# Two chained cross-head projections: TensorE as four 64x64 arrays, data laid out by halves, column matrices kept in SBUF, the result added in place

## What is computed

```
ret  = einsum('BGMTS,GMN->BGNTS', x, w + eye)
hq   = einsum('BGMTS,BTGIM->BGITS', x, qw1);  ret += einsum('BGITS,BTGIM->BGMTS', hq, qw2)
hk   = einsum('BGMTS,BSGIM->BGITS', x, kw1);  ret += einsum('BGITS,BSGIM->BGMTS', hk, kw2)
ret += x * qdd[t] + x * kdd[s]
```

## Time and profile before

| | |
|---|---|
| median of three runs | 987.55 us |
| profiled execution | 987.69 us, of which the span of the instructions is 985.8 us |
| TensorE (matmul) | 946.6 us busy, 96% of the span |
| VectorE / GpSimd / ScalarE | 748.4 / 715.7 / 319.2 us busy |
| DMA | 159.74 MB, 16 engines busy 50.5% of the span by queue q1 |

### The profile page before, as it was taken

The page is one execution under the profiler, slowest core; times in us unless marked ns, Lnnn a source line. Parts: engine busy times, 40 slices in busy tenths (PEclk is TensorE's granted clock), DMA queues, the critical chain, the costliest instruction groups (busy, mean ns, idle before and its releaser), DMA issues.

```text
span 985.8 us, 24446 instructions
## 1 busy us (share of the span) xinstructions
PE 946.6 (96%) x8378; PEld 939.4 (95%) x8378; DVE 748.4 (76%) x1036; ACT 319.2 (32%) x514; POOL 715.7 (73%) x603
## 2 busy tenths in 40 slices
PE   3679999999999999999999999999999999999998
PEld 3669999999999999999999999999999999999998
DVE  3996767787777876788677886779767786778997
ACT  0234333323333333333333233333333333333320
POOL 2998876678766976669866787668876697665666
PEclk8789999999999999999999999999999999999999
DMA  8952118770386506872088702866048730784017
GB/s 214 328 142 61 16 47 296 258 185 1 129 292 240 125 1 210 287 245 43 1 288 288 202 6 86 282 253 164 1 167 286 255 73 1 243 293 128 1 44 299
DMA packets 76493, 159.74 MB, mean 162 GB/s; under 512 B 39936, under 2 KB 40960, under 8 KB 73856
## 3 DMA queue, kind: packets, MB, share of 16 engines
q1 hardware_dynamic: 76416, 158.54, 50.5%
HBM read 89.19 MB, written 69.34 MB: 161 GB/s over the span
## 4 chain that ended last, share of the span: by engine, by line
PE 88%; POOL 7%; DMA 2%; issue 2%; POOLq 1%; DVE 0%
PE PB L482 24%; PE PA L482 23%; PE PA L488 21%; PE PB L488 20%; POOL WA L160 3%; POOL PROD L265 2%; DMA RT<-products 2%; POOL PROD L269 1%; DMA products<-RT 1%; POOL PROD L272 0%; DVE WA L448 0%; POOLq L288 0%; POOLq L160 0%; DVE RT L375 0%; POOLq L283 0%
## 5 line engine op out<-in xcount | busy, mean ns | idle before, releaser
L160 POOL TENSOR_TENSOR WA<-RT,mask 128x512 f32<-128x512 f32 x277 | 341.9, 1242 | 151.1 <-PE PA L482 121.2
L160 POOL TENSOR_TENSOR WA<-RS,mask 128x512 f32<-128x512 f32 x256 | 328.2, 1292 | 104.8 <-PE PA L488 87.3
L482 PE MATMUL PA<-X,WA 128*128 128x128 f32 x2048 | 281.9, 280 | 26.4 <-POOL WA L160 19.5
L482 PEld LDWEIGHTS PA<-X,WA 128*128 128x128 f32 x2048 | 257.2, 192 | 31.5 <-issue 23.9
L405 DVE TENSOR_TENSOR OUT<-PB,X 128x512 f32<-128x512 f32 x256 | 176.0, 691 | 131.2 <-PE PB L482 130.0
L488 PE MATMUL PA<-Y,WA 128*128 128x128 f32 x2048 | 267.9, 272 | 5.9 <-POOL WA L160 5.9
L488 PE MATMUL PB<-X,WB 128*128 128x128 f32 x2048 | 267.5, 272 | 0.0
L338 ACT ACTIVATE Y<-PA 128x512 f32<-128x512 f32 (+1 forms) x256 | 162.1, 633 | 321.6 <-PE PA L482 321.6
L344 ACT ACTIVATE X<-PA 128x512 f32 x256 | 155.6, 608 | 311.1 <-PE PA L488 311.1
L488 PEld LDWEIGHTS PA<-Y,WA 128*128 128x128 f32 x2048 | 247.2, 188 | 7.3 <-POOL WA L160 7.2
L482 PE MATMUL PB<-Y,WB 128*128 128x128 f32 x1880 | 250.3, 274 | 0.0
(11 more groups left out here) (32 smaller groups left out, 62.9 us busy)
## 6 DMA issues: line engine op xcount, KB each, us to landing
X<-in_x_dram SPq DMA_DIRECT2D x128, 512.0 KB, 4.9
out_dram<-OUT SPq DMA_DIRECT2D x128, 512.0 KB, 3.1
RT<-products SPq DMA_DIRECT2D x16, 1024.0 KB, 11.8
OUT<-in_right_dram SPq DMA_DIRECT2D x2, 1024.0 KB, 11.0
products<-PROD SPq DMA_DIRECT2D x16, 128.0 KB, 4.1
Y<-in_right_dram SPq DMA_DIRECT2D x1, 1024.0 KB, 22.9
X<-in_right_dram SPq DMA_DIRECT2D x1, 1024.0 KB, 26.8
QP<-in_rows_dram SPq DMA_DIRECT2D x8, 80.0 KB, 3.4
```

Of the source, the lines that this page charges most:

```text
L160: engine.tensor_tensor(dst, r, m, ALU.mult).then_inc(ready, 1)
L482: last = nc.tensor.matmul(bank[:, r, :], weights[:, r].rearrange("q n p -> q (n p)"), row(buf, pair, r), start=True, stop=True)
```

## The change

TensorE is addressed as four 64x64 arrays: input half h (partitions 0 to 63 or 64 to 127) and output half o. The partitions now hold 2 halves x 4 parts x 16 channels. The row tile of 64 partitions is multiplied by a 64x64 matrix with 4 repeats. Each former matmul of 128 moving columns becomes four of 64 (one per array), which together cover the same row. The results of the two input halves go to two PSUM banks, those of the output halves to the two halves of the partitions.

```
+            def four(banks, at, weights, moving, full=None):
+                for h in range(HALVES):
+                    inside = slice(HALF * h, HALF * (h + 1))
+                    for o in range(HALVES):
+                        rhs = moving(inside, o)
+                        dst = banks[h][HALF * o:HALF * (o + 1), ROWS * at:ROWS * (at + 1)]
...
+                        last = nc.tensor.matmul(dst, weights(inside, o), rhs, start=True, stop=True)
+                if full is not None:
+                    last.then_inc(full, 1)
+            def multiply_rows(banks, weights, rows, full):
+                for r in range(CHUNK):
+                    four(banks, r,
+                         lambda inside, o: weights[inside, r].rearrange("q a n -> q (a n)"),
+                         lambda inside, o: rows[inside, r // PAIR, WIDE * o:WIDE * (o + 1), r % PAIR],
+                         full if r == CHUNK - 1 else None)
```

```
+            def t1_copies(k, e, j):
+                act.wait_ge(a_full, before_t1(k) + j + 1)
+                for h in range(HALVES):
+                    nc.scalar.activation(half_rows(y_rows(e, j), h), by_rows(PA[j % RING][h]), ACT.Copy
+                                         ).then_inc(a_done, 1)
+            def add_rows(k, e, o):
+                dve.wait_ge(b_full, before_t2(k) + o + 1)
+                dve.wait_ge(a_done, copied(before_t1(k + 1)))
+                for h in range(HALVES):
+                    at = half_rows(x_rows(e, t2_chunk(o)), h)
+                    nc.vector.tensor_tensor(at, by_rows(PB[o % RING][h]), at, ALU.add).then_inc(b_done, 1)
```

VectorE only adds from now on. The expanded column matrices RSX are made once and stay in SBUF: layer 1 by ScalarE (16 copies scaled by the mask), layer 2 by GpSimd (4 spreads of 128x2048). GpSimd makes all row matrices, t1's into WA and t2's into WB, in turn, and forms the products once per two blocks, in the middle of the first of the two t phases:

```
+            def turn(m, first, more):
+                k = 2 * m
+                for j in range(CHUNKS):
+                    t1_weights(k + 1, j, False)
+                    t2_weights(k, j, first)
+                    if j == SLOTS - 1 and more:
+                        products_of(m + 1, False)
```

The compact column matrices are formed in 16 units: TensorE broadcasts the k2 values into PSUM by a matmul with a selection matrix (`fill`), VectorE multiplies and adds (`column_unit`), onto a base that GpSimd (layer 1) and ScalarE (layer 2) make. X is double (X[0], X[1]); t2 is added in place into X, stored from there, and the chunk of the block after next is loaded into the same place once the store has landed:

```
+                def reload(o):
+                    j = t2_chunk(o)
+                    sp.wait_ge(stored[j], DMA * (k + 1))
+                    load_x(k + 2, e, j)
+                for o in range(CHUNKS):
+                    sp.wait_ge(b_done, copied(before_t2(k) + o + 1))
+                    store(k, e, t2_chunk(o))
+                    if more and o >= BEHIND:
+                        reload(o - BEHIND)
```

More of the change, by code:

```diff
@@ L21 @@
 CHUNK2 = CHUNK // PAIR
-PER_CHUNK = CHUNK // GRP
-SLACK = 3
+PAIRS = ROWS // PAIR
+SLACK = 1
+RING = 2
 SLOTS = 4
+LAG = 2
+BEHIND = 3
+QUARTERS = 4
+QUARTER = COLS // QUARTERS
+NARROW = QUARTER // HALVES
+UNITS = LAYERS * QUARTERS * RANK
+FILLS = 4
 PARAMS = 2 * RANK * CH + CH
@@ L27 @@
 FLAT = CHUNK * COLS
[L28 to L32, removed]
+BANK = 512
 def cross_conv_kernel(nc, x, first_rows, row_params, col_left, col_right, w, products, out):
@@ L153, in by_columns, with column_index @@
         def by_columns(bank):
[L154 to L159, removed]
+            return bank[:, :].rearrange("q (s a c) -> q s a c", s=CHUNK, c=PAIR)
+        def column_index(o, v):
+            return QUARTER * (v // NARROW) + NARROW * o + v % NARROW
@@ L226, in _ @@
[L226 to L232, removed]
-            sp.wait_ge(first_stored, DMA)
-            load_rt(BLOCKS, 0)
-            load_x(0, 2)
-            load_x(0, 3)
@@ L257, in _ @@
+            load_rt(1, 0, 1)
+            with sp.Fori(0, TURNS - 2) as m:
+                turn(m, True)
+                load_q(m + 2)
+            turn(TURNS - 2, True)
+            turn(TURNS - 1, False)
+            for j in range(CHUNKS):
+                sp.wait_ge(stored[j], DMA * BLOCKS)
         @block.gpsimd
@@ L280, in products_of @@
                     row_matrices(l, (RANK + 1) * (LAYERS * step + l))
-            def phase(compact, before, start, end, there, count):
-                with pool.Fori(start, end) as it:
-                    pool.wait_ge(there, count)
-                    for i in range(RING):
-                        pool.wait_ge(a_full, before + RING * it + i - RING + 1)
-                        spread(nc.gpsimd, WA[:, i], compact, GRP * (RING * it + i), wa_ready)
-            def s2_weights(k, more):
-                if more:
-                    phase(RS[:, 1], before_s2(k), 0, PROD_TURN, rs_ready, LAYERS)
-                    products_of(k + 1)
-                    phase(RS[:, 1], before_s2(k), PROD_TURN, GROUPS // RING, rs_ready, LAYERS)
-                else:
-                    phase(RS[:, 1], before_s2(k), 0, GROUPS // RING, rs_ready, LAYERS)
@@ new lines, in s2_copies @@
+            def s2_copies(k, e, g):
+                act.wait_ge(a_full, before_s2(k) + g + 1)
+                for h in range(HALVES):
+                    nc.scalar.activation(half_columns(X[e], h, g), by_columns(PA[g % RING][h]), ACT.Copy
+                                         ).then_inc(a_done, 1)
+            act.wait_ge(wi_ready, LAYERS)
+            base(1)
+            for j in range(CHUNKS):
+                t1_copies(0, 0, j)
+                if j % 2:
+                    column_spread(j // 2)
@@ new lines, in turn @@
+            def turn(m, more):
+                k = 2 * m
+                for g in range(CHUNKS):
+                    s2_copies(k, 0, g)
+                for j in range(CHUNKS):
+                    t1_copies(k + 1, 1, j)
+                for g in range(CHUNKS):
+                    s2_copies(k + 1, 1, g)
+                if more:
+                    for j in range(CHUNKS):
+                        t1_copies(k + 2, 0, j)
+            with act.Fori(0, TURNS - 1) as m:
+                turn(m, True)
@@ L472, in _ @@
         @block.tensor
         def _(pe):
-            def row(buf, pair, r):
-                return buf[:, bass.ds(pair + r // PAIR, 1), :, r % PAIR:r % PAIR + 1].rearrange("q a s c -> q (a s c)")
-            def column(buf, k, s):
-                return buf[:, bass.ds(pair_place(k), ROWS // PAIR), bass.ds(s, 1), :].rearrange("q a s c -> q (a s) c")
-            def multiply_rows(bank, weights, buf, pair, full):
-                for r in range(GRP):
-                    last = nc.tensor.matmul(bank[:, r, :], weights[:, r].rearrange("q n p -> q (n p)"),
-                                            row(buf, pair, r), start=True, stop=True)
-                last.then_inc(full, 1)
@@ L486, in multiply_columns @@
-            def multiply_columns(bank, weights, buf, k, g, full):
-                for r in range(GRP):
-                    last = nc.tensor.matmul(bank[:, r, :].rearrange("q (a c) -> q a c", c=PAIR),
-                                            weights[:, r].rearrange("q n p -> q (n p)"),
-                                            column(buf, k, GRP * g + r), start=True, stop=True)
-                last.then_inc(full, 1)
-            def t1(k, g):
-                j = g // PER_CHUNK
-                if g % PER_CHUNK == 0:
-                    pe.wait_ge(x_loaded[j], DMA * (k + 1))
-                pe.wait_ge(wa_ready, before_t1(k) + g + 1)
-                if not (first(k) and g < RING):
-                    pe.wait_ge(a_done, before_t1(k) + g - RING + 1)
-                multiply_rows(PA[g % RING], WA[:, g % RING], X,
-                              pair_at(k, j) + GRP // PAIR * (g % PER_CHUNK), a_full)
```

606 lines of the change are left out of this document (295 added, 311 removed).

## The result

| | before | after |
|---|---|---|
| median of four runs | 987.63 us (987.11 to 987.84) | 1129.31 us (1128.75 to 1129.98) |
| ratio | | 1.1436, 95% interval 1.1416 to 1.1456 |
| span of the profiled execution | 985.8 us | 1128.2 us |
| TensorE busy | 946.6 us | 713.7 us |
| instruction packets (16 KB each) | 69 | 257 |

The forecast was 587 us, with a range of 555 to 680. The rival that came true is the third, instruction supply, which I had given 0.04, half of it for a kernel slower than before.

The account below looks back on a forecast made before the run. TensorE was taken as the bound, at 0.118 us a row: 81 us start + 256.5 for 15 s phases + 211.4 for 14 t phases + 20 for RT + 16 end + 1.9 outside the span, 587 us; range 555 to 680.

Parts of the forecast that it names:

- rival 3: TensorE's instruction fetch: 16 KB packets one at a time could limit; about 1240 us at 4.9 us latency; chance 0.04.
- The formula: Whole kernel if fetch-bound: 97 + 232 L us for page latency L, slower than before from L > 3.8 us.
- the start and the end: First t phase ends at 81 us, set by ScalarE and GpSimd; the last t2 adds 16 us through VectorE.
- The second argument: Against instruction supply as the limit: the warm-up had no gap, though it was short.
- The s phase: TensorE's 15.1 us at 14.8 ns a record plus stalls of RING = 2: 17.1 us each, fifteen making 256.5 us.
- RT's way: RT loads queue behind stores on SyncE, delaying GpSimd's spreads in t phases: 20 us in all, ends 0 and 65.
- the signs: What would show the forecast: among others, 2048 matmul records in 15 us, 14.8 ns apart, in mid-phase.
- 481 us of transfers: DMA queues: about 154 MB at 320 GB/s, given as about 86% of the span after; it fits, barely.
- the spacing of 14.8 ns: TensorE's 64x64 matmuls start 14.8 ns apart at strides 1 and 2: 0.118 us a row, 483 us for all.
- rival 2: TensorE: a floor of 25 ns between matmuls, 0.2 us a row, 25.6 us a phase, 869 us; chance 0.04.
- rival 4: TensorE: with data the arrays work one after the other, 0.45 us a row, 1850 us; chance 0.01.
- the other engines' prices: GpSimd 1.07 us a spread, VectorE 0.69 an addition, ScalarE 0.61 to 0.63 a copy.

Follow-up runs that it names:

- looped kernel: Changed kernel with all matmuls from block 1 on reading one fixed place and each phase's groups in loops on TensorE; 804.46 us, 0.8145 of before.
- the mix: The kernel before, with its blocks of 128 rows, on four 64x64 arrays: row jobs 64 moving columns, column jobs 128; 980.95 us, 0.9946 of before.
- second experiment: Changed kernel with as many matmuls, each on 128 moving columns instead of 64, so twice the columns streamed; 1112.72 us, 1.1266 of before.

## Why the prediction was wrong

- **The step that failed** is the dismissal of rival 3. I had its mechanism, its formula and its threshold: slower than before from a latency of 3.8 us. Against it I set "1.1 us is below 1.9": the time that a packet takes on the DMA engines beside the 1.9 us of work in a page. That compares a part with the whole. My own sign of being wrong, gaps every 256 instructions, is what came. From page to page it is 4.23 us, of which the packet is 1.10 us, 1.39 us pass between its end and TensorE's next instruction, and the remaining 1.7 us lie ahead of the packet. Nothing in the trace of before shows that latency: there a page is 14 us of work, and TensorE has no wait put down to issue after the first 73 us. It was an unknown that needed bounds from both sides, and the upper one, the 4.9 us of a load of x, stood in my own text with 1240 us beside it.
- **The formula, with what was measured.** 97 + 232 x 4.23 = 1078 us, 5% under 1129; the 25 pages of the start and the end, which I had costed by the other engines, were fetch-bound too: the first t phase ended at 118 us where I had 81.
- **The second argument**, no stop in the warm-up, could not bear anything: the stretch read was 0.35 us long, 32 records and their weight loads, a quarter of a page. And the trace of before has the first packet of queue q8 at 15.86 us, after the whole warm-up: its instructions had come before, and no stop could show. The Trainium skill, Runtime: NRT & Kernel Launch, section Instruction fetch mechanics, describes pages fetched ahead by a queue of their own; the runs agree on the size and the queue. What ahead is worth they show too. With 2.1 us of work in a page TensorE stopped at nearly every page, with 3.5 us at about half of them. In the trace of after the next packet starts no sooner than 1.03 us after TensorE has gone on from a stop, with two exceptions (median 1.6 us): a page's packet comes while the page before it is worked on, and nothing here shows one further ahead.
- **Mis-sized terms beside the cause.** The s phase: 18.0 ns instead of 14.8 is 16384 records x 3.2 = 52 us; the price had come from a warm-up with strides 1 and 2 only. With that the sum would be 639 us. The looped kernel gives an estimate of a kernel without stops, though with near columns everywhere: 804.5 less the 170 us between records over 0.6 us apart (106 times after the first 36 us), 634 us; and 616.69 us were measured with half the instructions and little traffic. By these the sum was some 5 to 9% low, inside the range; the missing supply took it out.
- **RT's way** (20 us, up to 65) can't be read from after, where a slow TensorE hides it. In the kernels with half the instructions TensorE waits 38.0 + 6.2 = 44 us for x and GpSimd, and 17.4 + 3.2 = 21 us with little traffic. So the size was about right, but not the way: I had put it down to GpSimd's spreads behind RT, and it is nearly all x behind RT in SyncE's queue.
- **Where the time went.** TensorE's records at the spacings of the two windows are 256 pages x 2.1 = 538 us where before had 923, as meant. The other 545 us of 256 x 4.23 = 1083 are not all stops: after the first 36 us records over 0.6 us apart make 458 us (248 times). Most of what remains I put down, as an estimate, to records at half clock, which by its mean of 0.892 was granted for 22% of the span.
- **Slips in the sums.** TensorE's matmul records in a phase are 1024, not the 2048 of the signs (those are all instructions, with the weight loads); 481 us of transfers are 82% of 585, not 86%. Nothing in the forecast rests on either.

**Right** were the spacing of 14.8 ns (14.5 above in a t phase, 15.0 over whole stretches) against the 25 ns of rival 2, arrays that overlap against rival 4, and the other engines' prices, in these groups (busy us, mean ns, idle before):

```profile
L173 POOL TENSOR_TENSOR WA<-RT,mask 128x512 f32<-128x512 f32 x128 | 134.0, 1048 | 697.9 <-DMA RT<-products 467.5
L487 DVE TENSOR_TENSOR X<-PB,X 128x512 f32<-128x512 f32 x256 | 165.0, 687 | 451.8 <-PE PB L515 445.6
...
L401 ACT ACTIVATE X<-PA 128x512 f32<-128x512 f32 x256 | 141.1, 605 | 429.5 <-PE PA L515 428.5
```

1.05 us a spread (1.07 taken), 0.687 an addition, 0.605 a copy, against the earlier trace rows. GpSimd waits 467.5 us for RT, the longest wait of the kernel, and yet the chain has no POOL in it: the stores ahead of RT are late because TensorE is, and idle time of an engine that isn't the bound costs nothing.

**Left open:** what the time ahead of a packet is made of, and how traffic lengthens it (medians in after: 4.39 us a page at 100 GB/s and more, 3.76 below; mean in the mix 4.83). That the queue's requests line up behind others is an argument, not shown. Nor is it shown why the granted clock fell: it was 0.892 in after, 0.987 with twice the columns, and 0.992 with little traffic, where the stops were still there.

## What to carry to other kernels

Before you split an operation, work out how long the engine needs for 256 of its instructions; if that is well under 4 us, expect it to stop at most pages (2.1 us of work: at nearly every one; 3.5 us: at about half, and shorter; 14 us: at none), however good the price of one instruction looks, and put more columns into each instruction or run them from a loop. A kernel that never stops at a page says nothing of the latency there: such an unknown keeps its upper end in the range and isn't ruled out by the one part of it (the packet's own time) that the profile shows.

## What the hardware showed

- From page to page where TensorE's work is less: 3.72 us at a mean of 41 GB/s, 4.23 at 141 GB/s (the mix had 4.83 at 165 GB/s, with other waits among them).
- A float32 matmul on a 64x64 array: at full clock records start 14.5 (a window) to 15.0 ns apart (median of whole stretches) with 64 columns of near stride, 18.0 to 18.6 with strided ones, 27.4 ns with 128 columns (medians of the second experiment, in both phases); at half clock 26.9 ns with 64 columns.
- Instructions in a loop are executed again without being fetched: 32800 matmul records from 108 packets against 258.
- One broadcast load of 1 MB over 128 partitions landed in 15.57 us with the channels outermost and in 32.87 us with the repeats outermost, each beside loads of the k2 values in the same order (before and the mix).
